# Second expert FFN: the shared expert of blocks 6 and 7 behind the routed experts, their x^T in two slots outside the arena

## The chip, the cores and the metric

The kernel runs on one core of a Trainium2 chip. The metric is the time of one execution on the device in microseconds (us); lower is better. Five engines matter, each with an instruction stream of its own that meets the others at semaphores only: PE (TensorE, matmuls), DVE (VectorE), ACT (ScalarE), POOL (GpSimd) and SP (SyncE, which here only issues DMAs).

## The reference, cut to what matters

4 sequences of 1024 tokens of 128 features pass a mixture-of-experts FFN, a state-space mixer with a dense FFN, and the same mixture-of-experts FFN a second time.

```python
x = x + 0.5 * ffn(layernorm(x)); x = x + mixer(layernorm(x)); x = x + 0.5 * ffn(layernorm(x))

def ffn(x):                                  # 8 experts, 2 of them for each token
    shared = (silu(x @ sw1) * (x @ sw2)) @ sw3          # 128 -> 256 -> 128, all tokens
    w, idx = top_k(softmax(x @ rw + rb), 2); w = w / sum(w)
    routed = sum over k of w[k] * ((silu(x @ ew1[idx[k]]) * (x @ ew2[idx[k]])) @ ew3[idx[k]])
    return shared + routed
```

`shared` and `routed` of a token are independent of each other; both are added to the residual `x`.

## The kernel before

The 4096 tokens are 8 blocks (`NB`) of 512 (`BT`), a block being 4 tiles of 128 tokens. The residual `x` stays in SBUF for the whole program. A mixture-of-experts FFN (called "call 0" and "call 1"; a turn is call x 8 + block) has these parts:

- **Routing**, block by block: logits on PE, the two best experts and the row of each token in its expert's region on DVE (`dve_route`, `dve_places`). POOL then writes the normalised tokens to DRAM in expert order (`pool_scatter`, 8 indirect DMAs a block, L710). In call 1 the blocks 0 to 4 (`EARLY`) are routed inside the mixer; blocks 5 to 7 are routed beside the shared expert.
- **Shared expert**, block by block: `pe_xt` transposes the block into PSUM (L1963), `act_xt` copies it to one of four slots `xt_at` (L999), `pe_up` makes two pairs of 128x512 products (L2002 into `ps_a`, L2004 into `ps_b`), `act_silu` (L1006) and `dve_hid` (L1488) make the hidden values, `pe_down` multiplies them back (L2012), and `dve_shared` adds the result to `x` (L1493). The product behind it may only start once the sum before it is made.
- **Routed experts** in 36 pairs of 128-row tiles (`pe_experts`): SP loads the tiles from DRAM (L462, 8 buffers), PE transposes a pair (L2025), and the answers go from `dve_answer` (L1531) to POOL's indirect DMAs into DRAM by token (`pool_answers`, L726, two a pair).
- **The end**: when all answers are stored, SP loads them back by block (`y_in[1]`, L469), ACT scales one half (`act_finish`, L1042), and DVE adds both halves to `x` (`dve_finish`, L1551 and L1555), and SP stores each finished block (L472).

`arena` is one SBUF area used in phases: the 8 tile buffers, `y_in[1]` and two of the four `xt_at` slots (`xt_more`) share it. That is why SP, ahead of the first tile load, waits until the shared expert has read the last of its x^T (`b_ps_ready`, L455), and PE starts the routed experts only when the last shared block is added (`shared_added`). Slots 0 and 1 are `xt`, outside the arena.

Order is what each engine's function writes out by hand: nothing is scheduled by a tool. `pe_experts` is also what the order of the last turn hangs on: `pe_ffn_again` runs all eight blocks and then calls it.

Of the kernel before, what the change touches and what calls it, by code (L numbers as in the profile page):

```python
# [11 lines left out]
ACT = mybir.ActivationFunctionType  # L12

P = 128
TOK = 4096
BT = 512
NB = TOK // BT
TT = BT // P
HID = 256
NE = 8  # L20
NT = 2 * TOK // P + NE
NPAIR = NT // 2
# [6 lines left out]

EARLY = 5  # L30
BACK = (4, NB)
LN_EPS = 1e-5

NSEQ = 4
# [54 lines left out]
def macaron(nc, A, out):  # L89
    ctx = ExitStack()  # L90
    with ctx:
# [40 lines left out]
        w_shared = sb("w_shared", [P, 2 * HID])  # L132
# [52 lines left out]
        ps_a = ps("ps_a", [P, 2, BT])  # L185
# [12 lines left out]
        def ps_answers(p):  # L198
# [176 lines left out]
        (bc_raw_ready, bc_conv_ready, bc_rep_ready, logs_ready, h_added, rep_c_read, rep_b_read, mix_read) = (  # L375
            sem("m_" + n) for n in ("bc_raw", "bc_conv", "bc_rep", "logs", "h_added", "rep_c_read", "rep_b_read", "mix_read"))

        def after(eng, semaphore, value):

            if not (isinstance(value, int) and value <= 0):  # L380
                eng.wait_ge(semaphore, value)
# [28 lines left out]
        def _(sp):  # L410
# [33 lines left out]
            for call in range(2):  # L444

                sp.wait_ge(pads_ready, call + 1)
                pads = table(mybir.EngineType.SP, pad_row, 0, NE, DUMMY - P)
                for e in range(NE):
                    sp.dma_start(xs[bass.ds(pads[e], P), :], fill[:, :]).then_inc(pads_stored, 16)
                sp.wait_ge(tiles_ready, call + 1)  # L450
                at = list(table(mybir.EngineType.SP, row_at, 0, GROUP, DUMMY))
                sp.wait_ge(pads_stored, 16 * NE * (call + 1))
                sp.wait_ge(scattered, 16 * 2 * TOK // P * (call + 1))

                sp.wait_ge(b_ps_ready, 2 * NB * (call + 1))  # L455
                for i in range(NT):
                    if i and i % GROUP == 0:
                        at += list(table(mybir.EngineType.SP, row_at, i, min(GROUP, NT - i), DUMMY))
                    if i >= XIN:
                        sp.wait_ge(t_ps_ready, call * NPAIR + (i - XIN) // 2 + 1)  # L460
                        sp.wait_ge(dest_ready, call * NPAIR + (i - XIN) // 2 + 1)
                    sp.dma_start(x_tiles[:, i % XIN, :], xs[bass.ds(at[i], P), :]).then_inc(tile_in[i % XIN], 16)  # L462
                for r in range(YRING):
                    sp.wait_ge(y_stored[r], 32 * (NPAIR // YRING) * (call + 1))
                ring = BACK[call]
                for n in range(NB):
                    if n >= ring:
                        sp.wait_ge(combined, call * NB + n - ring + 1)
                    sp.dma_start(y_in[call][:, n % ring, :, :], yv[n]).then_inc(block_in[n], 16)  # L469
# [523 lines left out]

        def act_xt(act, turn):
            act.wait_ge(xt_ps_ready, turn + 1)
            if turn >= 4:

                act.wait_ge(b_ps_ready, 2 * (turn - 3))
            act.activation(xt_at[turn % 4], ps_t, ACT.Copy).then_inc(xt_ready, 1)  # L999

        def act_silu(act, turn, k):
            step = 2 * turn + k
# [31 lines left out]
                act.wait_ge(y_ps_ready, pair - 1)  # L1034
            act.activation(hid_t[:, p % 2, :], ps_d, ACT.Copy).then_inc(ht_ready, 1)  # L1035

        def act_finish(act):
            for n in range(NB):
                act.wait_ge(block_in[n], 16 * 3)
                for t in range(TT):  # L1040
                    second = y_in[1][:, n, t, P:2 * P]
                    r = act.activation(second, second, ACT.Copy, scale=share[:, 1, n * TT + t:n * TT + t + 1])  # L1042
                r.then_inc(second_scaled, 1)

        def act_ffn(act):
            act_xt(act, 0)
# [16 lines left out]
        def act_ffn_again(act):  # L1063
            act_xt(act, NB)
            act_xt(act, NB + 1)
            for n in range(NB):

                act_silu(act, NB + n, 0)
                if EARLY + n < NB:
                    act_route_xt(act, EARLY + n, ps_t)  # L1070
                act_silu(act, NB + n, 1)
                if n + 2 < NB:
                    act_xt(act, NB + n + 2)
            act_experts(act, 1)

        def act_experts(act, call):
            act_tanh(act, call)
# [10 lines left out]
        @block.scalar  # L1088
        def _(act):
            act_ffn(act)  # L1090
            act.wait_ge(mixer_const, MIXER_CONST)
            act_mixer(act)
            act_ffn_again(act)
            act_finish(act)


        def dve_mixer_const(dve):
# [505 lines left out]

        def dve_ffn_again(dve, own):
            dve.wait_ge(mixer_done, NB)
            for n in range(NB + 1):

                if n < NB:
                    dve_hid(dve, NB + n, 0)
                if 1 <= n <= NB - EARLY:  # L1610
                    dve_places(dve, own, NB + EARLY + n - 1)
                if n < NB:
                    dve_hid(dve, NB + n, 1)
                if n == 0:
                    dve_norm(dve, NB + NB - 1)
                if n:
                    dve_shared(dve, NB + n - 1)
                if n < NB - EARLY:
                    dve_route(dve, own, NB + EARLY + n)
                if n == NB - EARLY:  # L1620
                    dve_tiles(dve, own, 1)
            dve_experts(dve, own, 1)

        def dve_experts(dve, own, call):
            dve_gates(dve, own, call)
# [11 lines left out]
        @block.vector  # L1637
        def _(dve):
            own = Own(dve, own_dve)
            dve_ffn(dve, own)  # L1640
            dve_mixer(dve, lambda n: dve_combine(dve, own, 0, n), own)
            dve_ffn_again(dve, own)
            for n in range(NB):
                dve_finish(dve, own, n)


# [350 lines left out]
        def pe_up(pe, turn, k):  # L1997
            step = 2 * turn + k
            if step >= 2:
                pe.wait_ge(silu_done, step - 1)  # L2000
                pe.wait_ge(hid_done, step - 1)
            pe.matmul(ps_a[:, k, :], w_shared[:, k * P:(k + 1) * P], xt_at[turn % 4], start=True,  # L2002
                      stop=True).then_inc(a_ps_ready, 1)
            pe.matmul(ps_b[:, k, :], w_shared[:, HID + k * P:HID + (k + 1) * P], xt_at[turn % 4], start=True,  # L2004
                      stop=True).then_inc(b_ps_ready, 1)

        def pe_down(pe, turn):
# [90 lines left out]
        def pe_ffn_again(pe):  # L2098

            pe.wait_ge(mixer_done, NB)  # L2100
            pe.wait_ge(rank_read, NB + EARLY)
            pe_xt(pe, NB)
            pe_xt(pe, NB + 1)
            for n in range(NB + 1):

                late = EARLY + n
                if n < NB:
                    pe_up(pe, NB + n, 0)
                if late < NB:

                    pe.wait_ge(xt_ready, NB + n + 2)
                    pe_route_xt(pe, late, ps_t)
                if 0 <= n - 1 < NB - EARLY:

                    pe.wait_ge(rank_read, NB + late - 1)
                    pe_rank(pe, NB + late - 1)
                if n < NB:
                    pe_up(pe, NB + n, 1)
                if late < NB:

                    pe.wait_ge(logits_read, NB + late)
                    pe_route_logits(pe, late, ps_r)
                if n + 2 < NB:
                    if late < NB:
                        pe.wait_ge(rx_ready, late + 1)
                    pe_xt(pe, NB + n + 2)
                if n:
                    pe_down(pe, NB + n - 1)
            pe_experts(pe, 1)

        def pe_experts(pe, call):
            first = call * NB

            pe.wait_ge(which_ready, call + 1)
            which = list(table(mybir.EngineType.PE, tile_w, 0, GROUP, NE - 1))
            pe.wait_ge(shared_added, first + NB)
            if call == 0:
                pe.wait_ge(w_lo_ready, NE)
                pe.wait_ge(experts_down_in, 16 * NE)
            pe_tiles_t(pe, call, 0)  # L2140
            pe_tiles_t(pe, call, 1)
            for p in range(-1, NPAIR + 1):
                if p + 1 < NPAIR:
                    if p >= 0 and 2 * (p + 1) % GROUP == 0:
                        which += list(table(mybir.EngineType.PE, tile_w, 2 * (p + 1), min(GROUP, NT - 2 * (p + 1)), NE - 1))
                    pe_up_e(pe, call, p + 1, which)
                if 0 <= p < NPAIR:
                    pe_hid_t(pe, call, p)
                if p >= 1:
                    pe_down_e(pe, call, p - 1, which)  # L2150
                if p + 3 < NPAIR:
                    pe_tiles_t(pe, call, p + 3)

        @block.tensor
        def _(pe):
            pe.wait_ge(ident_ready, 3)
            pe_ffn(pe)
            pe_mixer_const(pe)
            pe_mixer(pe)
            pe_ffn_again(pe)  # L2160


_OUT_SHAPE = (NSEQ, SEQ, P)
# [44 lines left out]
```

## Time and profile before

| | |
|---|---|
| times of three runs | 786.61, 892.56, 2213.87 us |
| median | 892.56 us |
| span of the profiled execution | 783.3 us |
| mean granted clock of PE in it | 0.922 |
| busy: PE, DVE, ACT, POOL | 82%, 70%, 54%, 66% of the span |

The span runs from the first to the last instruction of one profiled execution; the profile gives no time of its own for that execution. The lowest of the three times is 3.3 us above its span. The whole of the change lies in the last 190 us: routing's end and the shared expert from 590 to 648 us, the routed experts from 648 to 756 us, the end from 756 to 783 us. The numbers in the text are positions on that profile's time axis.

### The profile page before, as it was taken

What the parts mean: (1) busy time and instruction counts of PE and PEld (TensorE: products, weight loads), DVE (VectorE), ACT (ScalarE), POOL (GpSimd) and SP (SyncE); (2) the same over time, 40 slices, a digit from 0 to 9 for tenths busy, and PEclk for the clock granted to TensorE, in tenths of its full rate; (3) what the DMA queues carried; (4) which work ended last, traced back from release to release, by engine and by line L of the source; (5) the groups of instructions that cost most, each with busy time, mean ns of one, the idle gap of its engine ahead of it and who ended that gap; (6) DMA issues with size and microseconds to landing.
All of it is one profiled execution on the core that took longest, in us unless ns stands there. A gap on an engine that the chain in (4) does not pass through costs nothing.

```text
span 783.3 us, 13708 instructions
## 1 busy us (share of the span) xinstructions
PE 644.3 (82%) x3768; PEld 475.4 (61%) x3768; DVE 547.1 (70%) x1706; ACT 424.9 (54%) x745; POOL 520.4 (66%) x656
## 2 busy tenths in 40 slices
PE   3478979999916288989999998999968999999950
PEld 2245558888812045656575756577635667888840
DVE  4666756666539659897989999999743645666637
ACT  1122225455406999998999998764212324545525
POOL 3787775666645676896978869686765713666660
PEclk9989989999966678999999999999988999999995
DMA  9411223333242000000000000000000212333219
GB/s 266 159 46 52 82 67 80 93 89 85 65 142 84 0 1 1 0 2 1 1 2 1 2 15 15 14 15 15 28 27 28 69 45 76 87 89 91 81 30 318
DMA packets 49368, 46.34 MB, mean 59 GB/s; under 512 B 8456, under 2 KB 42861, under 8 KB 49296
## 3 DMA queue, kind: packets, MB, share of 16 engines
q1 hardware_dynamic: 40592, 28.54, 13.0%
q0 software_dynamic: 8704, 16.93, 6.7%
q8 instruction: 34, 0.56, 0.3%
q14 instruction: 38, 0.31, 0.1%
HBM read 25.30 MB, written 21.19 MB: 59 GB/s over the span
## 4 chain that ended last, share of the span: by engine, by line
PE 35%; POOL 24%; issue 15%; DVE 13%; ACT 8%; DMA 4%; POOLq 1%; SPq 0%; DVEq 0%; ACTq 0%
POOL ys L726 11%; POOL xs L710 10%; PE ps_tr L1662 4%; PE ps_go L1662 3%; DMA xs<-rows,pos 2%; PE ps_tr L2064 2%; PE ps_go L2012 2%; PE ps_go L2051 1%; PE ps_go L1833 1%; PE ps_tr L1850 1%; PE ps_go L1837 1%; POOL rstd L700 1%; PE ps_b L1884 1%; PE ps_a L2002 1%; PE ps_go L1883 1%
## 5 line engine op out<-in xcount | busy, mean ns | idle before, releaser
L726 POOL DMA_INDIRECT ys<-arena,dest x144 | 141.0, 980 | 99.8 <-issue 65.4
L710 POOL DMA_INDIRECT xs<-rows,pos x128 | 127.2, 993 | 58.8 <-issue 35.8
L1006 ACT ACTIVATE silu_a<-ps_a 128x512 f32<-128x512 f32 x32 | 19.1, 597 | 62.1 <-PE ps_a L2002 62.1
L2064 PE MATMUL ps_tr<-w_down_e,arena 128*128 x384 | 50.7, 275 | 0.0
L1521 DVE TENSOR_TENSOR hid<-silu_a,ps_a 128x512 f32<-128x512 f32 x36 | 24.8, 688 | 34.1 <-ACT silu_a L1026 34.1
L1521 DVE TENSOR_TENSOR hid<-silu_a,ps_b 128x512 f32<-128x512 f32 x36 | 24.8, 688 | 34.1 <-ACT silu_a L1026 34.1
L2064 PEld LDWEIGHTS ps_tr<-w_down_e,arena 128*128 128x128 f32 x384 | 46.7, 192 | 0.0
L1035 ACT ACTIVATE arena<-ps_go 128x512 f32<-128x512 f32 x72 | 42.6, 592 | 2.0 <-PE ps_go L2051 2.0
L1488 DVE TENSOR_TENSOR hid<-silu_a,ps_b 128x512 f32<-128x512 f32 x32 | 21.9, 686 | 31.0 <-PE ps_b L2004 29.1
L2051 PE MATMUL ps_go<-ident,hid 128*128 128x128 f32 x288 | 43.2, 273 | 0.2
L1026 ACT ACTIVATE silu_a<-ps_a 128x512 f32<-128x512 f32 x36 | 21.5, 597 | 38.1 <-PE ps_a L2040 38.1
L1026 ACT ACTIVATE silu_a<-ps_b 128x512 f32<-128x512 f32 x36 | 21.5, 597 | 37.7 <-PE ps_b L2040 37.7
L2051 PEld LDWEIGHTS ps_go<-ident,hid 128*128 128x128 f32 x288 | 35.5, 140 | 10.1 <-DVE hid L1521 0.8
L1018 ACT ACTIVATE xt_hi<-ps_tr 128x256 fp32r<-128x256 f32 x48 | 18.5, 385 | 35.0 <-PE ps_tr L2025 35.0
L1833 PE MATMUL ps_go<-arena,state 128*128 128x128 f32 x128 | 31.3, 329 | 7.4 <-DVE us L1291 6.5
L2012 PEld LDWEIGHTS ps_go<-w_shared_down,hid 128*128 128x128 f32 x256 | 31.6, 197 | 7.6 <-issue 7.6
L1963 PE MATMUL ps_tr<-ident,rows 128*128 128x128 f32 x64 | 13.5, 349 | 25.7 <-DVE rows L1404 19.9
L2012 PE MATMUL ps_go<-w_shared_down,hid 128*128 128x128 f32 x256 | 32.1, 280 | 1.7 <-DVE x L1493 1.7
L1833 PEld LDWEIGHTS ps_go<-arena,state 128*128 128x128 f32 x128 | 21.5, 201 | 19.4 <-issue 13.9
L2038 PE MATMUL ps_a<-up_hi,xt_hi 128*128 x72 | 31.8, 442 | 0.9 <-DVE xt_lo L1506 0.8
L1662 PE MATMUL ps_go<-arena,w_tap 128*128 128x512 f32 x64 | 32.2, 649 | 0.0
L2038 PE MATMUL ps_b<-up_hi,xt_hi 128*128 x72 | 31.6, 439 | 0.0
(368 smaller groups left out, 2032.5 us busy)
## 6 DMA issues: line engine op xcount, KB each, us to landing
arena<-xs SPq DMA_DIRECT2D x144, 65.0 KB, 1.9
rows<-ys SPq DMA_DIRECT2D x8, 512.0 KB, 3.7
arena<-ys SPq DMA_DIRECT2D x8, 512.0 KB, 6.8
ys<-arena,dest POOLq DMA_INDIRECT x144
x<-in_L_attn_x SPq DMA_DIRECT2D x8, 256.0 KB, 4.4
arena<-in_L_ffn_ew SPq DMA_DIRECT2D x4, 512.0 KB, 6.9
xs<-rows,pos POOLq DMA_INDIRECT x128
out<-x SPq DMA_DIRECT2D x8, 256.0 KB, 4.7
```

What stands on the lines that cost most here:

```text
L710: pool.indirect_dma_start(xs, bass.IndirectOffsetOnAxis(pos[:, n, i:i + 1], 0), rows[:, n * TT + i % TT, :], None).then_inc(scattered, 16)
L726: pool.indirect_dma_start(ys, bass.IndirectOffsetOnAxis(dest[:, i:i + 1], 0), y_out[:, p % YRING, j, :], None, bounds_check=2 * TOK - 1, o ...
L1026: act.activation(silu_a[:, p % 2, :].rearrange("p (j h) -> p j h", j=2), ps_pair[p % 2][:, :, 0:HID], ACT.Silu).then_inc(silu_e_done, 1)
L1035: act.activation(hid_t[:, p % 2, :], ps_d, ACT.Copy).then_inc(ht_ready, 1)
L1488: dve.tensor_tensor(hid[:, turn % 2, k, :], silu_a[:, k, :], ps_b[:, k, :], ALU.mult).then_inc(hid_done, 1)
L1521: dve.tensor_tensor(hid[:, p % 2, 0, :].rearrange("p (j h) -> p j h", j=2), silu_a[:, p % 2, :].rearrange("p (j h) -> p j h", j=2), ps_pai ...
L1662: r = pe.matmul(target, weights(k), zt[:, shift:shift + BT], start=(k == 0), stop=(k == taps - 1))
L1833: pe.matmul(pb["o"][:, at], state[:, k % 2, p * P:(p + 1) * P], cfs[:, q, k * P:(k + 1) * P], start=True, stop=False)
L2012: r = pe.matmul(ps_d[:, t * P:(t + 1) * P], hid[:, turn % 2, k, t * P:(t + 1) * P], w_shared_down[:, k, :], start=(k == 0), stop=(k == 1))
L2038: pe.matmul(target, xt_hi[:, p % 2, mine], hi, start=True, stop=False)
L2051: r = pe.transpose(ps_d[:, at:at + P], hid[:, p % 2, 0, at:at + P], ident[:, :])
L2064: r = pe.matmul(ps_answers(p)[:, j * P:(j + 1) * P], hid_t[:, p % 2, at:at + P], w_down_e[:, bass.ds(which[2 * p + j], 1), k, :].rearrange ...
```

## The change

In call 1 the loops of the shared expert on PE, ACT and DVE run over blocks 0 to 5 (`AHEAD`) and the routed experts follow. Blocks 6 and 7 (`LATE`) come behind the routed experts (`pe_late`, `act_late`, `dve_late`). PE starts them when the last answer has been copied (`answer_ready`). Their x^T goes to the two slots in `xt`. SP's wait for `b_ps_ready` and PE's for `shared_added` ask for two blocks fewer. On ACT and DVE the end's operations stand among the late ones: DVE adds the answers of block 0 after the late shared sum of block 6, and then the shared sum of block 7 ahead of the answers of block 1.

```diff
+LATE = 2
+AHEAD = NB - LATE
...
+        def xt_slot(turn):
+            return xt_at[turn % 4 if turn < NB + AHEAD else turn % 2]
...
-                sp.wait_ge(b_ps_ready, 2 * NB * (call + 1))
+                sp.wait_ge(b_ps_ready, 2 * (NB, NB + AHEAD)[call])
...
         def act_xt(act, turn):
             act.wait_ge(xt_ps_ready, turn + 1)
-            if turn >= 4:
+            if turn >= NB + AHEAD:
+
+                act.wait_ge(b_ps_ready, 2 * (turn - 1))
+            elif turn >= 4:
...
-            act.activation(xt_at[turn % 4], ps_t, ACT.Copy).then_inc(xt_ready, 1)
+            act.activation(xt_slot(turn), ps_t, ACT.Copy).then_inc(xt_ready, 1)
...
+        def act_late(act):
+
+            act_xt(act, NB + AHEAD)
+            act_xt(act, NB + AHEAD + 1)
+            for n in range(AHEAD, NB):
+                act_silu(act, NB + n, 0)
+                act_silu(act, NB + n, 1)
+                if n + 2 < NB:
+                    act_xt(act, NB + n + 2)
+                if n > AHEAD:
+                    act_finish(act, n - AHEAD - 1)
+            for n in range(LATE - 1, NB):
+                act_finish(act, n)
...
+        def dve_late(dve, n):
+
+            for k in range(2):
+                if n < NB:
+                    dve_hid(dve, NB + n, k)
+            if n > AHEAD:
+                dve_shared(dve, NB + n - 1)
...
             dve_ffn_again(dve, own)
+            dve_late(dve, AHEAD)
             for n in range(NB):
+
+                if AHEAD + n < NB:
+                    dve_late(dve, AHEAD + n + 1)
                 dve_finish(dve, own, n)
...
+        def pe_late(pe):
+
+            pe.wait_ge(answer_ready, 2 * NPAIR)
+            pe_xt(pe, NB + AHEAD)
+            pe_xt(pe, NB + AHEAD + 1)
+            for n in range(AHEAD, NB + 1):
+                for k in range(2):
+                    if n < NB:
+                        pe_up(pe, NB + n, k)
+                if n + 2 < NB:
+                    pe_xt(pe, NB + n + 2)
+                if n > AHEAD:
+                    pe_down(pe, NB + n - 1)
...
         def pe_experts(pe, call):
-            first = call * NB
-
...
-            pe.wait_ge(shared_added, first + NB)
+            pe.wait_ge(shared_added, (NB, NB + AHEAD)[call])
```

PE, where call 1's shared expert ends and its routed experts begin. L1963 is a transpose to x^T, L2002 and L2004 are the products into `ps_a` and `ps_b`, L2012 the product back (8 matmuls a block), L2025 the first transposes of the routed experts. Before:

```order
L1963 MATMUL ps_tr<-ident,rows 128x128 x4
L2012 MATMUL ps_go<-w_shared_down,hid 128x128 x8
L2002 MATMUL ps_a<-arena,w_shared 128x512
L2004 MATMUL ps_b<-arena,w_shared 128x512
L2002 MATMUL ps_a<-arena,w_shared 128x512
L2004 MATMUL ps_b<-arena,w_shared 128x512
L2012 MATMUL ps_go<-w_shared_down,hid 128x128 x8
```

After it follow four more products and the last two blocks' L2012 (16 in a row), then L2025. In the changed kernel the same engine has, with L2036, L2038 and L2046 for L2002, L2004 and L2012, and L2059 for L2025:

```order
L2036 MATMUL ps_a<-xt,w_shared 128x512
L2038 MATMUL ps_b<-xt,w_shared 128x512
L2036 MATMUL ps_a<-xt,w_shared 128x512
L2038 MATMUL ps_b<-xt,w_shared 128x512
L2046 MATMUL ps_go<-w_shared_down,hid 128x128 x16
L409 TENSOR_LOAD tile_w
L2059 MATMUL ps_tr<-ident,arena 128x128 x2
```

The `ps_a<-arena` and `ps_b<-arena` products of blocks 6 and 7, and the transposes of these blocks, are gone from here. They stand at PE's end, behind the last products of the routed experts, where PE had nothing before:

```order
L2098 MATMUL ps_go<-w_down_e,arena 128x128
L1997 MATMUL ps_tr<-ident,rows 128x128 x8
L2036 MATMUL ps_a<-xt,w_shared 128x512
L2038 MATMUL ps_b<-xt,w_shared 128x512
L2036 MATMUL ps_a<-xt,w_shared 128x512
L2038 MATMUL ps_b<-xt,w_shared 128x512
L2036 MATMUL ps_a<-xt,w_shared 128x512
L2038 MATMUL ps_b<-xt,w_shared 128x512
L2036 MATMUL ps_a<-xt,w_shared 128x512
L2038 MATMUL ps_b<-xt,w_shared 128x512
L2046 MATMUL ps_go<-w_shared_down,hid 128x128 x16
```

DVE at its end in the changed kernel; before, the rows L1553 (the answers' copies) were followed at once by L1573 and L1577 (the final sums, L1551 and L1555 in the kernel before):

```order
L1553 COPY arena<-ps_go 128x256
L1510 TENSOR_TENSOR hid<-silu_a,ps_b 128x512 x4
L1515 TENSOR_TENSOR x<-x,ps_go 128x512
L1573 SCALAR_TENSOR_TENSOR x<-arena,share,x 128x128 x4
L1577 TENSOR_TENSOR x<-x,arena 128x512
L1515 TENSOR_TENSOR x<-x,ps_go 128x512
L1573 SCALAR_TENSOR_TENSOR x<-arena,share,x 128x128 x4
```

Four hidden products and the first shared sum now stand ahead of the first final sum, and the second shared sum ahead of the second. The orders of POOL and SP are the same in both kernels.

## Rows read from the trace of the kernel before

**Rows 1.** The page: span, busy times, clock of TensorE in slices

```profile
span 783.3 us, 13708 instructions
...
PEclk9989989999966678999999999999988999999995
```

**Rows 2.** Timeline of PE around the start of the experts: start, length (us)

```profile
631.32 0.60 PE L1963 MATMUL ps_tr<-ident,rows 128*128 128x128 f32 x4
631.75 1.95 PE L2012 MATMUL ps_go<-w_shared_down,hid 128*128 128x128 f32 x16
633.54 1.02 PE L2002 MATMUL ps_a<-arena,w_shared 128*128 128x512 f32 x2
634.40 1.02 PE L2004 MATMUL ps_b<-arena,w_shared 128*128 128x512 f32 x2
...
645.01 2.02 PE L2012 MATMUL ps_go<-w_shared_down,hid 128*128 128x128 f32 x16 [0.87 <-DVE x L1493]
647.82 0.44 PE L2025 MATMUL ps_tr<-ident,arena 128*128 128x128 f32 x2 [0.78 <-DVE x L1493]
```

**Rows 3.** Timeline of DVE, same stretch

```profile
633.74 0.69 DVE L1493 TENSOR_TENSOR x<-x,ps_go 128x512 f32<-128x512 f32 x1 [1.48 <-PE ps_go L2012]
...
644.18 0.69 DVE L1493 TENSOR_TENSOR x<-x,ps_go 128x512 f32<-128x512 f32 x1 [1.04 <-PE ps_go L2012]
647.08 0.69 DVE L1493 TENSOR_TENSOR x<-x,ps_go 128x512 f32<-128x512 f32 x1 [2.21 <-PE ps_go L2012]
```

**Rows 4.** Timeline of ACT: the copy of x^T of block 7

```profile
631.95 0.60 ACT L999 ACTIVATE arena<-ps_tr 128x512 f32<-128x512 f32 x1 [0.70 <-PE ps_tr L1963]
```

**Rows 5.** Timeline of POOL: first and last of 24 scatters in a row

```profile
601.11 1.09 POOL L710 DMA_INDIRECT xs<-rows,pos  x1 [4.89 <-DVE pos L1451]
...
630.33 0.96 POOL L710 DMA_INDIRECT xs<-rows,pos  x1 [0.30 <-issue]
```

**Rows 6.** Chain of waits, in order of time: a scatter's landing

```profile
589.47 2.34 DMA xs<-rows,pos
```

**Rows 7.** Waits of the DMA queue of SP, 600 to 662 us

```profile
SPq L455 <- PE ps_b L2004: 13.8, 1, 13.8
```

**Rows 8.** Timeline of SP's queue from 642.5 us: the first two tile loads

```profile
642.59 0.89 SPq L462 DMA_DIRECT2D arena<-xs  x2
```

**Rows 9.** The tile loads by themselves: from issue to landing

```profile
DMA to landing us min/median/max: 1.7/1.9/3.6
```

**Rows 10.** Windows: length, busy us of each engine, clock, DMA

```profile
601.00:603.00 2.00, 2.00 (x4) 0.70 (x3) 0.00 (x0) 0.60 (x1) 1.59 (x2) 0.50 0.10 33
...
644.00:647.00 3.00, 2.13 (x18) 1.86 (x16) 0.69 (x1) 0.00 (x0) 0.00 (x0) 1.00 0.53 122
647.00:650.00 3.00, 1.42 (x8) 1.07 (x8) 2.14 (x9) 0.66 (x2) 0.00 (x0) 1.00 0.15 34
```

**Rows 11.** Timeline of PE: a pause, and matmuls behind it

```profile
599.53 0.18 PE L1989 MATMUL ps_go<-chosen,earlier 128*128 128x32 bf16 x1 [3.28 <-DVE chosen L1434]
...
599.73 1.74 PE L2002 MATMUL ps_a<-xt,w_shared 128*128 128x512 f32 x2
601.26 1.91 PE L2004 MATMUL ps_b<-xt,w_shared 128*128 128x512 f32 x2
```

**Rows 12.** Timeline of DVE, last answers and the final sums

```profile
755.32 0.42 DVE L1531 COPY arena<-ps_go 128x256 f32<-128x256 f32 x1 [0.61 <-PE ps_go L2064]
766.14 1.14 DVE L1551 SCALAR_TENSOR_TENSOR x<-arena,share,x 128x128 f32<-128x128 f32 x4 [10.40 <-DMA arena<-ys]
767.45 0.69 DVE L1555 TENSOR_TENSOR x<-x,arena 128x512 f32<-128x512 f32 x1 [0.17 <-ACT arena L1042]
...
779.88 0.69 DVE L1555 TENSOR_TENSOR x<-x,arena 128x512 f32<-128x512 f32 x1
```

**Rows 13.** Chain of waits, the end: last scatter, loads of the answers

```profile
760.36 2.12 DMA ys<-arena,dest
...
762.56 3.49 DMA arena<-ys
```

More of the change, by code:

```diff
@@ L1035, in act_hid_t, with act_finish @@
             act.activation(hid_t[:, p % 2, :], ps_d, ACT.Copy).then_inc(ht_ready, 1)
[L1037 to L1043, printed above, removed]
+        def act_finish(act, n):
+            act.wait_ge(block_in[n], 16 * 3)
+            for t in range(TT):
+                second = y_in[1][:, n, t, P:2 * P]
+                r = act.activation(second, second, ACT.Copy, scale=share[:, 1, n * TT + t:n * TT + t + 1])
+            r.then_inc(second_scaled, 1)
         def act_ffn(act):
@@ L1065, in act_ffn_again @@
             act_xt(act, NB + 1)
-            for n in range(NB):
+            for n in range(AHEAD):
                 act_silu(act, NB + n, 0)
@@ L1071, in act_ffn_again @@
                 act_silu(act, NB + n, 1)
+                if n + 2 < AHEAD:
+                    act_xt(act, NB + n + 2)
+            act_experts(act, 1)
+        def act_late(act):
[4 more added lines that the diff above has]
+                act_silu(act, NB + n, 1)
                 if n + 2 < NB:
                     act_xt(act, NB + n + 2)
-            act_experts(act, 1)
+                if n > AHEAD:
+                    act_finish(act, n - AHEAD - 1)
+            for n in range(LATE - 1, NB):
+                act_finish(act, n)
         def act_experts(act, call):
@@ L1093, in _ @@
             act_ffn_again(act)
-            act_finish(act)
+            act_late(act)
         def dve_mixer_const(dve):
@@ L1605, in dve_ffn_again @@
             dve.wait_ge(mixer_done, NB)
-            for n in range(NB + 1):
-                if n < NB:
+            for n in range(AHEAD + 1):
+                if n < AHEAD:
                     dve_hid(dve, NB + n, 0)
@@ L1611, in dve_ffn_again @@
                     dve_places(dve, own, NB + EARLY + n - 1)
-                if n < NB:
+                if n < AHEAD:
                     dve_hid(dve, NB + n, 1)
@@ L2001, in pe_up @@
                 pe.wait_ge(hid_done, step - 1)
-            pe.matmul(ps_a[:, k, :], w_shared[:, k * P:(k + 1) * P], xt_at[turn % 4], start=True,
+            pe.matmul(ps_a[:, k, :], w_shared[:, k * P:(k + 1) * P], xt_slot(turn), start=True,
                       stop=True).then_inc(a_ps_ready, 1)
-            pe.matmul(ps_b[:, k, :], w_shared[:, HID + k * P:HID + (k + 1) * P], xt_at[turn % 4], start=True,
+            pe.matmul(ps_b[:, k, :], w_shared[:, HID + k * P:HID + (k + 1) * P], xt_slot(turn), start=True,
                       stop=True).then_inc(b_ps_ready, 1)
@@ L2103, in pe_ffn_again @@
             pe_xt(pe, NB + 1)
-            for n in range(NB + 1):
+            for n in range(AHEAD + 1):
                 late = EARLY + n
-                if n < NB:
+                if n < AHEAD:
                     pe_up(pe, NB + n, 0)
@@ L2116, in pe_ffn_again @@
                     pe_rank(pe, NB + late - 1)
-                if n < NB:
+                if n < AHEAD:
                     pe_up(pe, NB + n, 1)
@@ L2122, in pe_ffn_again @@
                     pe_route_logits(pe, late, ps_r)
-                if n + 2 < NB:
+                if n + 2 < AHEAD:
                     if late < NB:
@@ L2160, in _ @@
             pe_ffn_again(pe)
+            pe_late(pe)
 _OUT_SHAPE = (NSEQ, SEQ, P)
```

## The prediction

> **What bounds the kernel now.** I read the page first, for the span and for PE's clock [rows 1], and then only the last 190 us, since the diff touches nothing ahead of 590 us. The timelines of PE and DVE at the start of the routed experts say what they wait for [rows 2, 3]. PE goes from matmul to matmul through the shared expert: it transposes block 7 at 631.32, does the product back of block 4 at 631.75 and the two-part products of blocks 6 and 7 from 633.54, and the transposes of the first expert pair start at 647.82, held by the last shared sum on DVE. So at this place the shared expert is the path. Two other things must be there too, POOL's scatters and SP's loads of the tiles. POOL issues 24 scatters from 601.11 to 630.33 in one go [rows 5], and SP waits on PE's `ps_b` for 13.8 us [rows 7] before its first load at 642.59 [rows 8]. Both have slack. From 647.82 on PE goes through 36 pairs; the copy of the last answer ends at 755.32 + 0.42 = 755.74 [rows 12]. I take these 107.9 us over unchanged: no instruction in them is touched. At the end PE is idle, the last scatter of POOL starts at 760.36, the answers' loads at 762.56 [rows 13], and DVE does the final sums from 766.14 to 779.88 + 0.69 = 780.57 with no wait between them to speak of [rows 12].
>
> **What is removed ahead of the experts.** Blocks 6 and 7 leave this place with their transposes, eight 128x512 products and two products back. The gain is the difference of two start times of the first expert pair, so I lay out the new one. Up to 631.32 nothing changes but a transpose of block 6, whose 0.4 us is swallowed: the products of block 5 waited for DVE's hidden values, which stand behind DVE's tile bookkeeping there. At 631.32, in place of the transposes of block 7, PE starts the product back of block 4. Its sum on DVE starts 633.74 - 631.75 = 1.99 us later, at 633.31 [rows 2, 3]. A product back that waits for the sum ahead starts 645.01 - 644.18 = 0.83 us after that sum's start: 634.14, for block 5. Its own sum starts 647.08 - 645.01 = 2.07 us on: 636.21. The expert pair follows 647.82 - 647.08 = 0.74 us later: 636.95. **Gain: 647.82 - 636.95 = 10.87 us.**
>
> **Does anything else hold the start?** SP's release by the x^T reads comes at 631.32, when the products of block 5 are over. The last scatter starts at 630.33 [rows 5]. A scatter landed 2.34 us after its start [rows 6], so this one by 632.67. At the end SP's load followed a scatter's landing by 762.56 - 760.36 - 2.12 = 0.08 us [rows 13], so the first load goes out at 632.8 and the second is out 0.89 us later [rows 8]. Landing takes 1.9 us in the median and 3.6 at most [rows 9]: tiles 0 and 1 are there at 635.6, or at 637.3 in the worst case, against 636.95. So the cost is 0 to 0.35 us; I take 0, the median's. The margin is only some 1.4 us: without the 24 scatters being over, no more blocks could be moved at a profit.
>
> **What is added behind the experts.** PE may start when the last answer is copied, at 755.74 on the old axis, plus the step from DVE to PE, 645.01 - 644.18 - 0.69 = 0.14: 755.88. The transposes of block 6; ACT's copy starts 631.95 - 631.32 = 0.63 later [rows 4], 756.51, and lasts 0.60: 757.11. Then, a tenth on, the transposes of block 7, 631.75 - 631.32 = 0.43: 757.63. Eight products at 634.40 - 633.54 = 0.86 [rows 2] make 6.88: 764.51. ACT's SiLU and DVE's hidden products run beside them, as they did for blocks 6 and 7 before, and the new wait of ACT (`b_ps_ready`, turn - 1) asks for block 5, long done. The product back of block 6 gives its sum a start at 764.51 + 1.99 = 766.50, and an end at 767.19. The final sum of block 0, queued behind this on DVE, started at 766.14 before. **It is 1.05 us late.** Block 7's product back starts at 767.19 + 0.14 = 767.33, its sum at 769.40. The final sum of block 0 takes one step of the cadence, (779.88 - 767.45) / 7 = 1.776 us [rows 12], to 768.97; DVE waits 0.43 and does the sum until 770.09. Seven more final sums end at 770.09 + 12.43 = 782.52, against 780.57. **Loss: 1.95 us.** ACT's scaling is not late, since its last SiLU is over before the loads land at 762.56 + 3.49 = 766.05 [rows 13].
>
> So nearly all of the 11.3 us from 755.88 to 767.19 is covered by POOL's last scatters, their landing and the loads; without that cover it would all be on the path. Bounds: 0, if PE were as quick as it takes to hide the rest; the upper end is the clock, below. Moving the DVE sums later by 1 to 2 us against the loads and the stores does nothing to the last store, which follows the last sum; I take the same 2.7 us from 780.57 to 783.3.
>
> **Sum.** -10.87 + 1.95 = -8.92 us: span 783.3 - 8.9 = 774.4 us. The lowest of the shown times is 786.61, 3.3 above the span, and I take that as what lies around it: **777.7 us**. The median shown, 892.56, is 106 us above; no row of the profile explains that, and the sum says nothing about it. The ratio, some 0.989, is what counts. A change of this kernel under 2% can hardly be told from none.
>
> **Rival 1: PE's clock falls in the late part (slower).** After 3.28 us of waiting for DVE at 599.53 the products of 599.73 and 601.26 have lengths of 1.74 and 1.91 us in place of 1.02 [rows 11], and the window from 601 reads a granted clock of 0.50, which is 1.2 of 2.4 GHz [rows 10]. The late part starts right behind a drain with little to do for PE, and has gaps of its own: 0.7 us for ACT's copy, 0.8 for the sum. With all of it at 0.50 the steps that are PE's double: transposes +0.4 twice, eight products +6.9, the products back +1.8 twice; together about 11.4 us more than in the sum above. That gives a span of 774.4 + 11.4 = 785.8, a time of 789.1. It decides from 8.9 us of extra on: with about four fifths of the late part at the low level the change loses. Against it: at 644 to 650 PE was busy 2.13 of 3.00 and 1.42 of 3.00 us, and the clock read 1.00 in both [rows 10], a sparser stretch than the late one. One low stretch as that from 599.73 to 603, two products at about +0.8, would cost 1.6 us: 779.3.
>
> The Trainium skill, page "TensorE: Matmul & The Clock Gate", section "A second HAM failure mode: psum-queue depth-cycling", speaks against this change: short idles between groups of matmuls can make the clock swing to its low level and back. By that rule the late part would pay rival 1's price; the windows at 644 to 650 had such idles and paid nothing.
>
> **Rival 2: the head gain does not come.** If the experts were held by what the change leaves alone (scatters, pads, tables), the first pair would stay near 647.8 and the 1.95 us would be added: span 785.3, time 788.6. The last scatter at 630.33 and SP's 13.8 us on `ps_b` [rows 5, 7] speak against it. A part of this, tile loads 3 us late, is 780.7.
>
> **Rival 3: the tail costs nothing.** If PE's late part ran 1 to 2 us shorter than my sum, by overlap of the second transpose and the copy, only the gain is left: 783.3 - 10.87 + 3.3 = 775.7.
>
> **How the numbers follow.** Forecast, 776.5 to 779: 0.64. One low stretch or loads a little late, 779 to 782: 0.12. Tail free, 774.5 to 776.5: 0.09. Most of the head gain lost, 782 to 788.6: 0.08. Clock low throughout, 789 and up: 0.05. Others, on either side: 0.02. The range of 774.5 to 785 holds about 0.88; the bound of the loads and half of rival 2 are in it. Faster by over 2% would need 770.9 and so more than the whole 10.87: 0.04. Slower by over 2% needs 802: 0.03. The rest, 0.93, is no change that can be told.
>
> **What the changed profile would show.** The first L2059 transposes (the old L2025) near 637; SP's first tile load near 633, on a scatter's landing; 107.9 us from the first pair to the last answer; late products from about 747 at clock 1.00 and 0.86 apart; DVE's first final sum right behind a shared sum and a wait of 0.4 us for block 7's; the last final sum about 771.7. I am wrong if the experts' pace changes, if a tile load is what PE waits for at 637, or if the late products stand 1.7 us apart.

## The result

The changed kernel takes 775.82 us in the median of four runs (775.01 to 776.47). Beside the kernel before on the same chip the ratio is 0.9877, 95% interval 0.9852 to 0.9901: 9.7 us shorter, with 7.8 to 11.6 in the interval. The profiled execution took 775.01 us with a span of 773.0. The forecast of 777.7 stood for a ratio of 0.989 against an execution of 786.6. Two later comparisons of the same two kernels gave 0.9884 (0.9858 to 0.9911) and 0.9886 (0.9867 to 0.9906); a third, told with the last experiment, gave 0.993 (0.9895 to 0.9965). The kernel before has a fourth time in this comparison, 785.39 us. The median of 892.56 us shown ahead and the 2213.87 beside it, as also one time of 1628.41 us of an experiment below (xt_ahead, second), belong to executions far longer than the others of the same kernel, and the ratios leave such runs out.

The page of the changed kernel, with the two lines that stand in [rows 1]:

```profile
span 773.0 us, 13708 instructions
...
PEclk9988999999976678979999999899997999999996
```

PE where the routed experts start (start, length in us); the old L2012, L2004 and L2025 are L2046, L2038 and L2059. The profile has two records for each matmul of these products, so the 8 of a product back are x16:

```profile
629.03 1.02 PE L2038 MATMUL ps_b<-xt,w_shared 128*128 128x512 f32 x2
629.89 1.95 PE L2046 MATMUL ps_go<-w_shared_down,hid 128*128 128x128 f32 x16
632.71 2.02 PE L2046 MATMUL ps_go<-w_shared_down,hid 128*128 128x128 f32 x16 [0.87 <-DVE x L1515]
635.51 0.44 PE L2059 MATMUL ps_tr<-ident,arena 128*128 128x128 f32 x2 [0.78 <-DVE x L1515]
...
636.38 0.33 PE L2059 MATMUL ps_go<-ident,arena 128*128 128x128 f32 x1 [0.32 <-DMA arena<-xs]
```

PE goes from the last of block 5's products, at 629.03, to the product back of block 4, waits for one sum, does block 5's, and has its first expert pair at 635.51, against 647.82 in [rows 2]. The distances are those of the sum (2.82 and 2.81): 2.82 us from one product back to the next, 2.80 to the pair. The last row is new: the fourth tile of the first two pairs arrived 0.32 us late. The first expert product follows the pair's transposes by 1.46 us in both profiles all the same.

SP's first load and the scatter that releases it:

```profile
630.16 0.96 POOL L716 DMA_INDIRECT xs<-rows,pos  x1 [0.30 <-issue]
...
632.75 3.47 SPq L468 DMA_DIRECT2D arena<-xs  x7
```

SP's row begins 2.6 us after the last scatter in place of 12.3 ([rows 5, 8]). The slack behind POOL is used up.

The end, on PE and on DVE (L1553 is the answer's copy, L1515 the shared sum, L1573 and L1577 the final sums):

```profile
743.49 0.65 PE L1997 MATMUL ps_tr<-ident,rows 128*128 128x128 f32 x4 [0.52 <-DVE arena L1553]
744.92 0.63 PE L1997 MATMUL ps_tr<-ident,rows 128*128 128x128 f32 x4 [0.78 <-ACT xt L1008]
745.39 1.02 PE L2036 MATMUL ps_a<-xt,w_shared 128*128 128x512 f32 x2
746.25 1.02 PE L2038 MATMUL ps_b<-xt,w_shared 128*128 128x512 f32 x2
...
752.26 1.95 PE L2046 MATMUL ps_go<-w_shared_down,hid 128*128 128x128 f32 x16
755.08 2.02 PE L2046 MATMUL ps_go<-w_shared_down,hid 128*128 128x128 f32 x16 [0.87 <-DVE x L1515]
...
743.01 0.42 DVE L1553 COPY arena<-ps_go 128x256 f32<-128x256 f32 x1 [0.61 <-PE ps_go L2098]
...
754.24 0.69 DVE L1515 TENSOR_TENSOR x<-x,ps_go 128x512 f32<-128x512 f32 x1 [1.04 <-PE ps_go L2046]
754.85 1.13 DVE L1573 SCALAR_TENSOR_TENSOR x<-arena,share,x 128x128 f32<-128x128 f32 x4
756.01 0.69 DVE L1577 TENSOR_TENSOR x<-x,arena 128x512 f32<-128x512 f32 x1
757.14 0.69 DVE L1515 TENSOR_TENSOR x<-x,ps_go 128x512 f32<-128x512 f32 x1 [0.43 <-PE ps_go L2046]
757.74 1.13 DVE L1573 SCALAR_TENSOR_TENSOR x<-arena,share,x 128x128 f32<-128x128 f32 x4
...
769.56 0.69 DVE L1577 TENSOR_TENSOR x<-x,arena 128x512 f32<-128x512 f32 x1
```

The late part begins 0.48 us after the last copy starts; its products stand 0.86 us apart, at the upper level of the clock; the first final sum waits for the shared sum of block 6, and block 7's comes in behind it after a pause of 0.43. From the last copy's start to the end of the last final sum it is 743.01 to 770.25, 27.24 us, against 755.32 to 780.57, 25.25 us, in [rows 12]: 1.99 us of loss, where the sum had 1.95.

The chain of waits says the same in another way. Before, it ran through POOL's last scatters and the loads of the answers ([rows 13]); now it goes through the late part:

```profile
743.01 0.44 DVE arena L1553
...
743.49 0.67 PE ps_tr L1997 x4
...
744.18 0.61 ACT xt L1008
...
752.42 1.80 PE ps_go L2046 x16
...
754.24 0.70 DVE x L1515
...
755.08 2.04 PE ps_go L2046 x16
...
757.74 1.14 DVE x L1573 x4
```

What does not fit is the total: the two profiled executions differ by 10.3 us, the sum has 8.9. The rest lies ahead of the change. Taken from the first of POOL's 24 scatters (601.11 and 600.97) the pair starts 46.71 us later before and 34.54 after, 12.2 less in place of 10.9. The windows of PE from 597 to 606 us (length, busy us of PE, PEld, DVE, ACT and POOL, clock, DMA), first of the kernel before, then of the changed one, tell why:

```profile
597.00:606.00 9.00, 6.47 (x38) 4.55 (x39) 4.30 (x27) 1.19 (x2) 3.97 (x4) 0.81 0.07 23
```

```profile
597.00:606.00 9.00, 6.87 (x47) 4.95 (x46) 5.36 (x34) 2.20 (x4) 3.97 (x4) 1.00 0.08 25
```

PE waits for DVE in front of the rank of block 5 in both, and not for the same time. In the kernel before it was 3.28 us ([rows 11]); this row stands ten microseconds ahead of it:

```profile
589.43 1.22 PE L2004 MATMUL ps_b<-xt,w_shared 128*128 128x512 f32 x2
```

In the changed kernel:

```profile
589.28 1.92 PE L2038 MATMUL ps_b<-xt,w_shared 128*128 128x512 f32 x2
...
599.39 0.18 PE L2023 MATMUL ps_go<-chosen,earlier 128*128 128x32 bf16 x1 [2.13 <-DVE chosen L1456]
```

The wait ends with DVE, so PE waits less where it comes later. In the changed kernel's profile the clock was still at 0.50 from 589 to 591, where the kernel before read 0.79, the second product there lasted 1.92 us in place of 1.22, and PE came later. Behind the wait of 3.28 us the granted clock fell (to 1.2 GHz of 2.4, [rows 10, 11]), behind that of 2.13 it did not. This is some 1.3 us. It lies ahead of the first instruction that the change moves, and the changed kernel's clock falls there too in another profiled execution, behind a wait of 3.41 us (below). How often it falls in either kernel is not shown; the profiles are too few.

### The profile page after: what moved, and what is told of

Read it like the earlier page. It is cut to its first block, busy times and chain, and to the rows that moved or that the text cites. A ratio compares the mean times of both kernels' runs of the same rounds, so it can differ in the third digit from the quotient of the medians.

```text
span 773.0 us, 13708 instructions
## 1 busy us (share of the span) xinstructions
PE 646.7 (84%) x3768; PEld 476.2 (62%) x3768; DVE 545.1 (71%) x1706; ACT 424.6 (55%) x745; POOL 520.0 (67%) x656
## 4 chain that ended last, share of the span: by engine, by line
PE 49%; POOL 16%; DVE 13%; issue 10%; ACT 8%; DMA 4%; SPq 0%; DVEq 0%; POOLq 0%; ACTq 0%
POOL xs L716 10%; PE ps_tr L2098 5%; PE ps_tr L1696 4%; PE ps_go L2085 4%; PE ps_go L1696 3%; PE ps_go L2098 2%; DMA xs<-rows,pos 2%; POOL ys L732 2%; PE ps_a L2072 2%; PE ps_a L2074 2%; PE ps_a L2073 2%; PE ps_b L2074 2%; PE ps_go L2046 2%; PE ps_b L2072 2%; PE ps_b L2073 2%
## 5 line engine op out<-in xcount | busy, mean ns | idle before, releaser
L2085 PEld LDWEIGHTS ps_go<-ident,hid 128*128 128x128 f32 x288 | 35.5, 140 | 10.2 <-DVE hid L1543 0.8
L2046 PEld LDWEIGHTS ps_go<-w_shared_down,hid 128*128 128x128 f32 x256 | 33.0, 203 | 10.1 <-issue 10.1
L2046 PE MATMUL ps_go<-w_shared_down,hid 128*128 128x128 f32 x256 | 33.2, 285 | 2.6 <-DVE x L1515 2.6
```

The source lines that it names most:

```text
L2046: r = pe.matmul(ps_d[:, t * P:(t + 1) * P], hid[:, turn % 2, k, t * P:(t + 1) * P], w_shared_down[:, k, :], start=(k == 0), stop=(k == 1))
L2085: r = pe.transpose(ps_d[:, at:at + P], hid[:, p % 2, 0, at:at + P], ident[:, :])
```

## The experiments

In all of them the ratio is to the kernel before, with its 95% interval. Positions within a profile are compared as distances, since the mixer ahead ends up to 2 us apart from execution to execution. Three distances come back below. "Head" is from POOL's first of the 24 scatters to the first expert pair. "Pairs" is from there to the start of the last answer's copy. "Tail" is from there to the start of the last final sum. "Wait" is PE's wait for DVE at the rank of block 5, near 599 us.

| kernel | ratio | head | pairs | tail | wait | clock 597 to 606 | clock 634 to 648 |
|---|---|---|---|---|---|---|---|
| before | 1 | 46.71 | 107.50 | 24.56 | 3.28 | 0.81 | 1.00 |
| changed | 0.9877 | 34.54 | 107.50 | 26.55 | 2.13 | 1.00 | 1.00 |
| changed, again | 0.9884 | 34.18 | 109.27 | 26.56 | 2.09 | 1.00 | 0.88 |
| changed, fourth | 0.9886 | 36.20 | 107.49 | 26.55 | 3.41 | 0.81 | 1.00 |
| block 7 alone moved | 0.9937 | 39.42 | 109.04 | 24.85 | 2.49 | 1.00 | 0.88 |
| blocks 5 to 7 moved | 0.9933 | 34.02 | 109.59 | 30.43 | 3.59 | 0.81 | 0.76 |
| late part left out | 0.985 | 34.53 | 107.51 | 24.80 | 2.11 | 1.00 | 1.00 |
| slots only, second | 0.9996 | 47.07 | 107.51 | 24.76 | 3.37 | 0.81 | 1.00 |
| x^T ahead, second | 0.9877 | 34.19 | 107.74 | 25.38 | 2.21 | 1.00 | 1.00 |
| two banks, second | 0.987 | 33.85 | 107.69 | 25.17 | 2.32 | 1.00 | 1.00 |

### The changed kernel again

No edit.

> The changed kernel as it is, as the measure for the three kernels beside it. Theory (10.87 us gained ahead of the routed experts, 1.95 us lost behind them): 8.9 us under the kernel before, a ratio of 0.9886, a span of about 773 to 774.4 us. Rival (the profiled execution of the changed kernel was only a lucky one, and its 10.3 us are all the change's): 10.3 us under, 0.987.

Measured: 0.9884, interval 0.9858 to 0.9911; 776.61 us beside 784.41, and a span of 774.8. This is the theory's number, but the rival's 0.987 lies in the interval too; what speaks against the rival is the changed kernel's fourth profile (last experiment). The tail is that of the first profile to 0.01 us. The pairs took 1.8 us more, and the place is the start of the experts:

```profile
636.00:638.00 2.00, 1.59 (x5) 0.97 (x6) 0.94 (x4) 0.77 (x2) 0.00 (x0) 0.79 0.60 131
638.00:640.00 2.00, 2.00 (x7) 1.42 (x6) 0.42 (x3) 0.00 (x0) 0.00 (x0) 0.50 0.52 119
640.00:642.00 2.00, 2.00 (x11) 1.69 (x10) 1.17 (x4) 0.87 (x2) 0.00 (x0) 0.85 0.21 51
```

```profile
637.24 0.79 PE L2072 MATMUL ps_a<-up_hi,xt_hi 128*128 x1
637.83 0.63 PE L2073 MATMUL ps_a<-up_lo,xt_hi 128*128 x1
...
640.95 0.39 PE L2074 MATMUL ps_b<-up_hi,xt_lo 128*128 x1
```

The clock falls to 0.50 from about 637 to 641 and the first expert products last 0.63 us in place of 0.39. A part of the 1.8 us, 0.26, comes of the tiles: here the first expert product follows the pair's transposes by 1.72 us in place of 1.46. So the clock does fall near this change, but at the head, behind the pauses at the seam, not in the late part of rival 1.

### How many blocks: one or three

```diff
-LATE = 2
+LATE = 1
```

For one block the second transposes of the late part go, and PE waits for the copy of the first ahead of its products.

> Only block 7 is moved (LATE = 1), with a wait of PE for its x^T. Theory: ahead of the experts one block less is removed, and the first pair starts 5.64 us earlier than before (of 10.87); behind them the one block is wholly under POOL's scatters and the loads (its sum would start at 762.6 on the old axis, the final sums at 766.1), so the tail costs 0. Net 5.6 us under the kernel before, 3.3 us over the changed kernel. Rival (each late block costs 0.98 us of tail, in proportion): net 4.7 us under.

Measured: 0.9937 (0.9912 to 0.9963), 4.9 us under the kernel before, 779.94 us. The head is 4.9 to 5.2 us longer than in the changed kernel at the same clock (39.42 to 34.54 and 34.18), where 5.23 was expected. The tail is 24.85, beside 24.56, 24.76 and 24.80 in the three profiles that have nothing late, so the one block is free. Its sum is done at 758.62, and the final sums wait 1.9 us more, for the loads:

```profile
757.93 0.69 DVE L1514 TENSOR_TENSOR x<-x,ps_go 128x512 f32<-128x512 f32 x1 [2.15 <-PE ps_go L2045]
760.51 1.14 DVE L1572 SCALAR_TENSOR_TENSOR x<-arena,share,x 128x128 f32<-128x128 f32 x4 [1.90 <-DMA arena<-ys]
```

In this profile the clock fell at the start of the experts as well, and the pairs took 1.5 us more. The rival, 0.98 us of tail for each block, is out by the tail; the ratio alone could not tell 4.7 from 5.6.

```diff
-LATE = 2
+LATE = 3
```

> Blocks 5 to 7 are moved (LATE = 3), in the same two slots. Theory: PE is ready for the first pair about 5 us earlier than in the changed kernel but the last scatter and the tile loads hold it, so the head gains 1.5 us more only; the tail loses 5.9 us in place of 1.95, since 3.9 us of the third block have no cover. Net 6.5 us under the kernel before, 2.4 us over the changed kernel, and the first transposes wait for a DMA for about 3 us. Rival (nothing but the shared expert holds the start): head gains 5.2 us more, net 10.2 us under the kernel before, under the changed kernel by 1.3.

Measured: 0.9933 (0.9907 to 0.9958), 5.3 us under the kernel before, 780.24 us. This is where the two theories differ most, by 3.7 us, and the rival's 10.2 is outside the interval. The head is 2.2 us shorter than the changed kernel's at the same lower clock (34.02 and 36.20; 1.5 was expected), not 5.2, and PE waits for the tiles for 4.43 us:

```profile
635.80 0.79 PE L2059 MATMUL ps_tr<-ident,arena 128*128 128x128 f32 x2 [4.43 <-DMA arena<-xs]
...
630.08 0.96 POOL xs L716
...
631.34 2.28 DMA xs<-rows,pos
```

The tail is 30.43, 5.87 us over the kernel before; the sum had 5.9. In this profile the head gave 0.7 us more than expected, and the pairs took 2.1 us more, which the expectation did not have: behind the long wait the clock is at 0.50 when the experts start. This is about what the gain is short of the 6.5 us. Of one, two and three blocks two is the best count here, because POOL's last scatter allows no earlier start and the cover at the end is spent.

### The late part left out

```diff
-            pe_late(pe)
...
-            act_late(act)
+            for n in range(NB):
+                act_finish(act, n)
...
-            dve_late(dve, AHEAD)
...
-                if AHEAD + n < NB:
-                    dve_late(dve, AHEAD + n + 1)
```

> The shared expert of blocks 6 and 7 of the second FFN is left out altogether, with nothing in its place; the rest is the changed kernel. This measures what the late part costs on the path. Theory: 1.95 us less than the changed kernel, 10.9 us under the kernel before, and the first final sum starts when the first load has landed. Rival (late part free): the same time as the changed kernel. Rival (the late part's DVE and DMA neighbours also slow the loads or stores): more than 3 us less.

Measured: 0.985 (0.9825 to 0.9875), 773.04 us, 2.7 us under the changed kernel by the ratios, whose intervals overlap. The tail decides: 24.80 in place of 26.55, so the late part costs 1.75 us of the path. That is neither free nor over 3. The first final sum again waits for a DMA:

```profile
741.92 0.42 DVE L1554 COPY arena<-ps_go 128x256 f32<-128x256 f32 x1 [0.61 <-PE ps_go L2096]
752.98 1.14 DVE L1574 SCALAR_TENSOR_TENSOR x<-arena,share,x 128x128 f32<-128x128 f32 x4 [10.63 <-DMA arena<-ys]
```

### The slots without the move

The kernel before, with `xt_slot`, the wait of `act_xt` and the wait of SP of the change, and nothing else of it.

> Only a part of the change: x^T of blocks 6 and 7 goes to the two slots outside the arena and SP's first tile loads wait for two blocks fewer, but the shared expert of both blocks stays ahead of the routed experts. Theory (the gain is the start of the first pair, and PE's own work holds it): SP's first load is issued near 633 in place of 642.6, the first pair still starts at its old distance behind the last product, and the time is that of the kernel before, within 0.5 us. Rival (early loads are a part of the gain): 1 to 2 us under it.

> slots_only once more, for the same reason. Theory: the time of the kernel before within 0.5 us, with SP's first tile load near 633 and the first pair near 647. Rival: 1 to 2 us under it.

Measured first in a comparison in which all four kernels and the kernel before were some 70 us longer (854.28 us for the kernel before): 1.0004 (0.9976 to 1.0032). The second one, at the usual times: 0.9996 (0.9982 to 1.001), 784.94 us beside 785.07. SP's first load went out at 632.14, ten microseconds earlier, and the first pair started after the last sum as ever, head 47.07 at the lower clock:

```profile
632.14 18.87 SPq L468 DMA_DIRECT2D arena<-xs  x12
...
647.19 0.44 PE L2034 MATMUL ps_tr<-ident,arena 128*128 128x128 f32 x2 [0.78 <-DVE x L1502]
```

The early loads are worth nothing alone. That the move needs them is read from the code and was not run: SP's old wait asks for the products of all eight blocks, two of which now stand behind the experts.

### x^T ahead of the experts

The transposes of block 6 stay where they were, those of block 7 go behind the product back of block 4, into the pause before the next; PE waits for both copies ahead of the first pair. ACT's copies move with the transposes (not shown below).

```diff
-                if n + 2 < AHEAD:
+                if n + 2 < NB - 1:
                     ...
                     pe_xt(pe, NB + n + 2)
                 if n:
                     pe_down(pe, NB + n - 1)
+                if n + 2 == NB - 1:
+                    pe_xt(pe, NB + n + 2)
+            pe.wait_ge(xt_ready, 2 * NB)
             pe_experts(pe, 1)
...
         def pe_late(pe):
-            pe_xt(pe, NB + AHEAD)
-            pe_xt(pe, NB + AHEAD + 1)
```

> The changed kernel, with the transposes and copies of x^T of blocks 6 and 7 left ahead of the routed experts, in pauses that PE has there anyway; the late part begins with the products. Theory: the first pair starts as in the changed kernel, the first late sum is ready at 764.8 on the old axis, 1.4 us ahead of the first final sum, so that only the second late sum (0.6 to 0.7 us) stays on the path. Tail loss 0.65 in place of 1.95: 1.3 us under the changed kernel, 10.2 under the kernel before, a ratio of 0.987. Distances: last answer's copy to first final sum 10.8 to 11.1 us (11.84 in the changed kernel), first to last final sum 14.35 (14.71). Rival (the late part waits for something else than its own length, the landing of the loads): no change against the changed kernel.

> xt_ahead once more, since all kernels of its comparison, the kernel before among them, were some 70 us longer than in the first one, with waits of several us strewn over all engines. Theory as there: 1.3 us under the changed kernel, a ratio of 0.987 to the kernel before, 10.8 to 11.1 us from the last answer's copy to the first final sum. Rival: no change against the changed kernel.

Measured: 0.9917 (0.9886 to 0.9948) in the long comparison, where the changed kernel had 0.993; 0.9877 (0.9856 to 0.9899) in the second, where it had 0.9886. By the ratios this is 0.7 to 1.1 us, and the intervals don't tell it from none. By the rows it is plain: from the last copy to the first final sum 744.32 to 755.30, 10.98 us in place of 11.84, and from the first to the last 14.40 in place of 14.71; the tail is 25.38, 1.17 us shorter. The pairs are 0.24 us longer, since two of the first tiles came 0.21 us late. The shared sum of block 6 is now early, and DVE waits for the loads:

```profile
753.76 0.69 DVE L1511 TENSOR_TENSOR x<-x,ps_go 128x512 f32<-128x512 f32 x1 [1.04 <-PE ps_go L2042]
755.30 1.14 DVE L1569 SCALAR_TENSOR_TENSOR x<-arena,share,x 128x128 f32<-128x128 f32 x4 [0.85 <-DMA arena<-ys]
...
757.29 0.68 DVE L1511 TENSOR_TENSOR x<-x,ps_go 128x512 f32<-128x512 f32 x1
```

### A second bank for the product back

```diff
+        TWO_BANKS = (NB + AHEAD - 1, 2 * NB - 1)
+        def down_bank(turn):
+            return ps_k if turn in TWO_BANKS else ps_d
...
-            after(pe, shared_added, turn)
+            after(pe, shared_added, turn - 1 if turn in TWO_BANKS else turn)
```

> xt_ahead, and the products back of block 5 and of block 7 go to a second PSUM bank, so that they need not wait for the sum ahead of them. Theory: ahead of the experts PE's pause of 0.87 us goes, of which the transposes of block 7 filled 0.43; the first pair starts 0.4 us earlier than in xt_ahead, nothing changes at the end: 0.4 us under xt_ahead. Rival (SP's tile loads, behind the last scatter, hold the start by then): no gain over xt_ahead, and a wait of PE for a DMA of 0.4 us and more at the first pair.

> two_banks once more, for the same reason. Theory: 0.4 us under xt_ahead, by an earlier first pair. Rival: the tile loads behind the last scatter hold the first pair, no gain.

Measured: 0.9908 (0.9875 to 0.994) in the long comparison and 0.987 (0.9849 to 0.9891) in the second, 773.69 us, the lowest median of all complete kernels. From block 5's first product to the first pair it is 626.31 to 634.77, 8.46 us, in place of 9.13 in xt_ahead (627.45 to 636.58): 0.67 us, a little more than expected. The rival is out: what PE waited for at the pair was still a sum. But the tiles are close behind: the first expert product follows by 1.65 us in place of 1.46, and the pairs are 0.2 us longer than in the changed kernel.

```profile
631.60 0.60 PE L1998 MATMUL ps_tr<-ident,rows 128*128 128x128 f32 x4
632.04 1.95 PE L2047 MATMUL ps_go<-w_shared_down,hid 128*128 128x128 f32 x16
634.77 0.64 PE L2060 MATMUL ps_tr<-ident,arena 128*128 128x128 f32 x2 [0.78 <-DVE x L1516]
```

The three distances make 168.59 us in the changed kernel and 166.71 here at the same clock, so that both steps together take 1.9 us off; the ratios, 0.9886 and 0.987 of one comparison, allow that and also none.

### The changed kernel twice more

> The changed kernel as it is, for the comparison with the three beside it: 8.9 us under the kernel before, a ratio of 0.9886. TensorE's granted clock after the pauses at 599 and at 636 us read 1.00 in one profiled execution of it and 0.50 at 638 in the other. Theory: this is chance from execution to execution and not the change's, so either can show here.

> The changed kernel as the measure for them: 0.9886 of the kernel before. Either level of TensorE's clock can show behind the pauses at 599 and 636 us.

Measured: 0.993 (0.9895 to 0.9965) in the long comparison, which is 6.0 us of 854.28 with 3.0 to 9.0 in the interval, and 0.9886 (0.9867 to 0.9906) in the last, 776.01 us. The fourth profile had the clock down at 601 as the kernel before, and its head is 36.20: against 46.71 of the kernel before at the same clock the head gains 10.51 us, and against slots_only_2, 47.07, 10.87. All three distances together are 170.24 us there, against 178.77 and 179.34 in these two: 8.5 and 9.1 us less at the same clock, where the sum has 8.9. So the 10.3 us between the first two profiles are not all the change's, and the rival of the second profile is out. The four profiles of the long comparison show waits that no profile at the usual times has, such as these of ACT in the changed kernel (waited for: us in total, times, longest):

```profile
ACT xt_hi L1027 <- remote: 44.7, 17, 3.3
```

Where the 70 us come from was not looked into further; all kernels had them.

## Why the prediction came out as it did

**What bounds the kernel** held. With the shared expert's two blocks out of the way the first pair came forward by what they took, and slots_only showed that the earlier loads alone do not bring it forward.

**The gain at the head**, 10.87 us, measured 10.5 to 10.9 at equal clock (the fourth profile against the two that have all eight blocks ahead). The 12.2 us between the first two profiles have 1.3 us of the clock near 599 in them. Each step of it stands in the profile after at its length, down to the 2.82 and 2.80 us between the rows.

**What else could hold the start** was right as a bound, and its slack was smaller than I had it: I put tiles 0 and 1 ahead of PE by 1.4 us and did not follow tiles 2 and 3, one of which came 0.32 us late. It cost nothing that the pairs' length shows there (107.50 in both) and 0.26 us in the changed kernel's second profile, within the 0 to 0.35 us of the text. By its own sign of being wrong, a tile load that PE waits for near 637, the text missed something, but it was small. late3 shows the wall itself.

**The loss at the tail**, 1.95 us, measured 1.99 against the kernel before and 1.75 against the late part left out. The order on DVE, the pause of 0.43 and the final sums behind it are as laid out.

**Rival 1**, the clock in the late part, did not come: the products stand 0.86 us apart, and the stretch from 744 to 757 reads 1.00 in the changed kernel's three profiles at the usual times. Behind it stood the rule of the Trainium skill, page "TensorE: Matmul & The Clock Gate", section "A second HAM failure mode: psum-queue depth-cycling". It is stated there for a bf16 kernel, and in the late part the traces do not bear it out. At the head of the experts the clock fell in three of the ten profiles of the table, at 1.5 to 2.1 us: in two of them (changed, again, and block 7 alone) behind short pauses, as by that rule, in the third behind a single wait of 4.43 us for the tiles. The prediction looked for it at the wrong seam. **Rivals 2 and 3** are out, the second by the pair at 635.51, the third by the tail.

**The step that failed is the last one, what the sum is set against.** "The lowest of the shown times is 786.61, 3.3 above the span, and I take that as what lies around it": in all executions on record that list both, the time is 1.7 to 2.1 us above the span, 2.0 in the changed kernel's profiled one (775.01 - 773.0). The 786.61 was another execution than the profiled one; the fourth time, 785.39, stands 2.1 us above the span of 783.3 and fits it. So some 1.3 us of the 777.7 were a wrong constant. With 2.0 the sum gives 776.4, and the medians of the changed kernel at the usual times are 775.82, 776.61 and 776.01. And the number on record, 777.7 us, reads as a fall of 12.9% beside the shown median of 892.56, while the ratio is 1.2%. The text said that the ratio was meant and that the sum says nothing about the median, but not that the median is no usual time of this kernel: 25 executions of the kernel before in two later comparisons took 783.0 to 787.1 us. The forecast of the change itself, 0.989, lies in every interval of the comparisons at the usual times.

**Luck.** The measured 775.82 falls into the band of 774.5 to 776.5, which the prediction gave to a free tail with 0.09, beside rival 3's 775.7, and not into its own of 776.5 to 779. The tail was not free; the number came there by the wrong constant. The chances also do not agree among themselves: 0.04 for under 770.9 is more than the 0.02 that the bands leave for everything outside them.

## What to carry to other kernels

Work that nothing downstream needs early can go behind a phase if it fits under the waits there: lay out its first result against the first thing that waits now, block by block: here the first block was free, the second cost 1.8 to 2.0 us and the third 3.9. Before counting the gain, list what else must be there at the earlier start (here POOL's last scatter and the loads behind it); that sets how much is worth moving. And compare profiles by distances between rows, not by positions or spans, when the effect is around 1%.

## What the runs showed of the hardware

PE's granted clock is not decided by the kernel alone, and whether it fell near 599 us went together with how long it had been low before. Near 590 us two 128x512 products follow each other in all ten profiles of the table. In four of them the second lasted 1.14 to 1.23 us, PE came early to its wait for DVE and waited 3.28 to 3.59 us, and the clock fell behind it (0.81 over 597 to 606). In the other six it lasted 1.91 or 1.92 us, PE came later and waited 2.09 to 2.49 us, and the clock stayed (1.00). The next rank came 1.3 to 1.8 us earlier in these six. The three profiles of the changed kernel at the usual times are on both sides (waits of 2.13, 2.09 and 3.41 us), so the kernel does not settle it. No run varies the wait by itself: this is what goes together, and not a cause shown.

At the seam where the experts start the clock fell in three of the ten, at 1.5 to 2.1 us. There the pauses do not tell the cases apart: the changed kernel's second profile had 0.92, 0.87, 0.78 and 0.28 us and the clock fell, its fourth had 1.07, 0.87, 0.78 and 0.80 and it read 1.00. Both falls are larger than the steps of this study below 1 us, and they make up most of what the changed kernel's profiled executions differ by.
